# An attention and feed-forward block: instruction orders without an engine loop, with the score chunks of both heads in runs

## Chip, core and metric

The kernel runs on one core of a Trainium2 chip. The metric is the device time in microseconds of one execution of the whole program, all input and weight loads included. Five engines work side by side, each through its own list of instructions: TensorE (PE), VectorE (DVE), ScalarE (ACT), GpSimd (POOL) and SyncE (SP). They wait for each other through semaphores.

## What is computed

The input x is 8 batches of 512 tokens with 256 features, all fp32:

```python
xn = layernorm(x)                                  # over the 256 features
q, k = rope(xn @ wq + bq), rope(xn @ wk + bk)      # 16 heads of 16 features
v = xn @ wv + bv
s = softmax(q @ k.T / 4 + causal mask) @ v @ wo + bo
g = silu((silu(xn @ wg.T) * (xn @ wu.T)) @ wd.T)   # 768 hidden, int32 weights / 127
out = x + s * g
```

For accuracy the kernel splits fp32 operands into a high part (fp32r) and a low part, and multiplies the parts separately.

## The kernel before

The work of each batch is cut into tokens, and for every engine an order of tokens is written out by hand. A token is a kind and an index: `A:3` is score chunk 3. The same token may stand in several engines' lists, and each engine does its own share of it: for `G:0` PE multiplies, ACT takes the tanh and DVE the product.

The kinds that take part below are these. `XT` transposes the normalised input. `QK` and `V` are projections (4 of each a batch), `ROPE` the rotation, `HI` and `LO` the high and low parts of q and k for a pair of heads. `T1q`, `T1k` transpose them into `q_st` and `k_st`. `A` is the first pass of scores of a pair, which DVE reduces to the maximum of each row (L778); `MX` puts the maximum into two more columns of q, `T2` transposes q again, and `B` is the second pass, from which ACT takes the exponential (L668) and POOL masks the diagonal blocks (L869). `PV` multiplies by the values, four heads and four steps, and `ON` normalises. `AT` and `OP` are the output projection, `G`, `U`, `DN` the feed-forward part (6, 6 and 2 a batch), `AD` adds x.

A pair has 6 chunks for each pass: 0 and 1 of 512 columns, 2 and 3 of 384 + 128 (two matmuls), 4 and 5 of 256. Even chunks belong to the first head of the pair, whose operands lie on partitions 0 to 63, odd ones to the second head, on 64 to 127 (`rows` in the matmul tokens, L551 and L562). `A` uses 48 of the 64 rows, `B` all. All other matmuls use all 128 rows; those of `PV` write 32 columns of the array each, four heads side by side.

`SCHEDULE` gives each engine one list of eight lines for a batch, a line for each pair. Kinds in `AHEAD` are shifted by whole pairs: in line s, `A` works on pair s + 1 and `B` on pair s - 1. A token with `>` belongs to the next batch, one with `<` to the batch before. `START` is the list ahead of the first batch.

Every result of PE except that of `PV` goes to one of seven PSUM banks, taken in rotation (`Bank`, `WORK_BANKS`); `take_bank` makes PE wait until the engine that empties the bank has released it. So PE can be at most seven tokens ahead of the slowest reader.

`run` writes plan -1 and plan 0 out, then `Fori` goes three times over plans 1 and 2 with the semaphore values worked out in registers (`need`), and plans 7 and 8 are written out again. SP has a loop of its own for the loads of x and the stores: it loads the x of the next batch behind `XT`, and stores `res` behind `AD`.

The sources of a few lines in the profile: L487 is every matmul of `QK`, `V`, `G`, `U`, `DN` and `OP`, L536 `T1q` and `T1k`, L542 `T2`, L554 `A`, L565 `B`, L580 `PV`, L589 `ON`.

Of the kernel before, what the change touches and what calls it, by code (L numbers as in the profile page):

```python
# [85 lines left out]
START = {
    "pe": """
        WQ XT:0 XT:1 WC V:0 QK:0 V:1 WT:0 QK:1 WT:1 WT:2 QK:2 WT:3 WT:4 V:2 WT:5 WT:6 V:3 QK:3 WT:7 WT:8 WT:9 WT:10 FLAG
        U:0 G:0 G:1 T1q:0 U:1 T1k:0 A:0 A:1 T1k:1 A:2 A:3 A:4 A:5 T1q:1
    """,  # L130
    "act": """
        WQ XT:0 XT:1 WC WT:0 WT:1 WT:2 WT:3 WT:4 WT:5 WT:6 WT:7 WT:8 WT:9 WT:10 G:0 HIq:0 G:1 HIq:1 T1q:0 HIq:2 HL:0
        T1k:0 T1k:1 T1q:1
    """,
    "dve": """
        WQ ST:0 NM:0 NM:1 NM:2 NM:3 XT:0 XT:1 WC V:0 QK:0 ROPE:0 ROPE:1 V:1 ROPE:2 SQ WT:0 ROPE:3 QK:1 ROPE:4 ROPE:5
        WT:1 WT:2 QK:2 ROPE:6 ROPE:7 WT:3 WT:4 V:2 WT:5 V:3 WT:6 WT:7 QK:3 WT:8 FLAG WT:9 WT:10 G:0 LOq:0 U:0 LOk:0 G:1
        U:1 HL:0 LOk:1 LOq:1 A:0 A:1 A:2 LOq:2 A:3 A:4 A:5 MX:0 LOk:2
    """,
    "pool": """  # L140
        WQ RS:0 WC SQ ROPE:8 ROPE:9 ROPE:10 ROPE:11 ROPE:12 ROPE:13 ROPE:14 ROPE:15 HIk:0 HIk:1 HIk:2
# [759 lines left out]
```

## Time and profile before

| | |
|---|---|
| median of 3 runs | 725.07 us (724.32 to 727.4) |
| profiled execution, span | 726.0 us |
| PE busy | 677.4 us, 93% |
| DVE busy | 538.6 us, 74% |
| ACT busy | 411.4 us, 57% |
| POOL busy | 351.7 us, 48% |
| mean granted clock of TensorE | 0.962 |

The profiled execution is one run of the program; its own time is the span of 726.0 us from the first to the last instruction, 0.9 us above the median of the runs and inside their spread. Busy time is time in which an engine works on at least one instruction. The ends of matmuls are modelled, so two neighbouring matmuls may overlap in the record; the distance from one start to the next is the safer measure. PEclk is the share of the full 2.4 GHz that TensorE was granted.

### The profile page before, as it was taken

The page shows a single profiled execution, that of the slowest core. Times are in us where ns is not written, and L with a number is a line of the kernel's source. Part 1 is how long each engine was busy: PE and PEld are TensorE (multiplying, and loading weights), DVE is VectorE, ACT ScalarE, POOL GpSimd, SP SyncE. Part 2 cuts the span into 40 slices and gives each one's busy share as a digit, 9 for nine tenths or more (in the row PEclk, how much of TensorE's full clock was granted, in tenths as well). Part 3 has the DMA queues.
Part 4 walks back from the last instruction along what each step waited for, and adds up shares of the span by engine and source line. Part 5 has one row for each costly group of instructions (what it writes and reads, how often), then busy time and mean ns, then how long its engine had stood idle before and what let it go on. Part 6 is the DMA issues. An engine that isn't in the chain of part 4 may idle for free.

```text
span 726.0 us, 15898 instructions
## 1 busy us (share of the span) xinstructions
PE 677.4 (93%) x4452; PEld 455.3 (63%) x4452; DVE 538.6 (74%) x1735; ACT 411.4 (57%) x897; POOL 351.7 (48%) x697
## 2 busy tenths in 40 slices
PE   1779999999999999899999999899999999999995
PEld 0656766676667665576656766568666766567653
DVE  3779678966978688675889669676697858886663
ACT  2446467756566447464476565555656644765671
POOL 1055493547625674336745476244762567422240
PEclk9888999999999999699999999879999999999898
DMA  8200000000100002000020001100020000100010
GB/s 247 78 1 1 31 1 1 2 3 1 62 28 1 1 1 89 6 1 2 1 89 2 2 1 59 35 2 3 1 74 16 1 1 2 60 1 1 1 60 29
DMA packets 16425, 18.15 MB, mean 25 GB/s; under 512 B 576, under 2 KB 15936, under 8 KB 16320
## 3 DMA queue, kind: packets, MB, share of 16 engines
q1 hardware_dynamic: 15232, 15.86, 6.8%
q8 instruction: 46, 0.75, 0.5%
q10 hardware_dynamic: 1088, 1.05, 0.4%
q14 instruction: 59, 0.48, 0.2%
HBM read 12.71 MB, written 4.19 MB: 23 GB/s over the span
## 4 chain that ended last, share of the span: by engine, by line
PE 84%; DVE 5%; issue 3%; ACT 3%; DMA 2%; POOL 1%; ACTq 0%; DVEq 0%; POOLq 0%
PE ps_w L487 34%; PE ps_w L565 12%; PE ps_w L554 12%; PE ps_o L580 11%; PE ps_w L536 7%; PE ps_w L542 3%; PE ps_w L589 3%; DMA rot<-L_attn_wo 2%; ACT probs L668 1%; PE ps_w L501 1%; ACT o_t L672 1%; DVE ps_w L778 1%; DVE h_lo L719 1%; PE ps_w L595 1%; DVE at_lo L801 1%
## 5 line engine op out<-in xcount | busy, mean ns | idle before, releaser
L778 DVE CUSTOM_DVE_ANT_0 ps_w<-ps_w,cst 128x512 f32<-128x512 f32 (+3 forms) x512 | 242.8, 509 | 54.5 <-PE ps_w L554 52.7
L668 ACT ACTIVATE probs<-ps_w 128x512 f32<-128x512 f32 (+1 forms) x384 | 194.1, 535 | 116.5 <-PE ps_w L565 113.6
L869 POOL TENSOR_SCALAR_AFFINE_SELECT probs<-probs 128x128 f32<-128x128 f32 (+1 forms) x384 | 130.7, 347 | 259.8 <-ACT probs L668 257.4
L565 PE MATMUL ps_w<-q_st,k_st 64*128 64x512 f32 (+3 forms) x512 | 137.9, 375 | 3.7 <-DVE at_lo L801 1.8
L554 PE MATMUL ps_w<-k_st,q_st 48*128 48x512 f32 (+3 forms) x512 | 139.3, 370 | 1.5 <-issue 0.8
L565 PEld LDWEIGHTS ps_w<-q_st,k_st 64*128 64x128 f32 x512 | 72.1, 189 | 52.9 <-issue 29.0
L658 ACT CAST q_st<-ps_w 128x512 fp32r<-128x512 f32 x128 | 74.6, 589 | 51.4 <-PE ps_w L542 39.3
L554 PEld LDWEIGHTS ps_w<-k_st,q_st 48*128 48x128 f32 x512 | 73.6, 189 | 47.3 <-issue 35.4
L487 PE MATMUL ps_w<-xt_hi,wgu_hi 128*128 128x512 f32 x192 | 89.3, 465 | 6.5 <-issue 4.8
L580 PE MATMUL ps_o<-probs,vals 128*32 128x512 f32 (+3 forms) x1024 | 92.5, 451 | 2.0 <-POOL probs L869 2.0
L487 PE MATMUL ps_w<-xt_lo,wgu_hi 128*128 128x512 f32 x192 | 80.7, 420 | 0.0
L778 DVE DVE_READ_ACCUMULATOR2_ANT row_max<- 128x1 f32 x512 | 72.1, 141 | 0.0
L684 ACT ACTIVATE hid<-ps_w 128x512 f32<-128x512 f32 x48 | 28.7, 598 | 54.1 <-PE ps_w L487 36.7
L407 POOL TENSOR_TENSOR rot<-qk_raw,cst 128x512 f32<-128x512 f32 x30 | 38.3, 1278 | 39.4 <-DVE qk_raw L745 32.4
L487 PEld LDWEIGHTS ps_w<-xt_hi,wgu_hi 128*128 128x128 f32 x192 | 38.2, 199 | 29.2 <-issue 18.0
L487 PE MATMUL ps_w<-w_hi,xt_hi 128*128 128x512 f32 (+1 forms) x128 | 50.1, 391 | 6.5 <-DVE w_lo L712 5.1
L814 DVE SCALAR_TENSOR_TENSOR hid<-hid,ps_w 128x512 f32<-128x512 f32 x48 | 32.8, 684 | 28.1 <-ACT hid L684 24.1
L487 PE MATMUL ps_w<-wd_hi,h_hi 128*128 128x256 f32 x192 | 47.9, 292 | 0.0
L658 ACT CAST k_st<-ps_w 128x512 fp32r<-128x512 f32 x64 | 38.5, 601 | 16.1 <-PE ps_w L536 15.9
L412 POOL TENSOR_TENSOR rope_b<-qk_raw,cst 128x256 f32<-128x256 f32 x56 | 47.2, 849 | 0.0
L487 PE MATMUL ps_w<-wd_hi,h_lo 128*128 128x256 f32 x192 | 46.1, 283 | 0.0
L487 PE MATMUL ps_w<-w_lo,xt_hi 128*128 128x512 f32 (+1 forms) x128 | 44.4, 347 | 0.0
(91 smaller groups left out, 1178.2 us busy)
## 6 DMA issues: line engine op xcount, KB each, us to landing
xn<-L_attn_x SPq DMA_DIRECT2D x8, 512.0 KB, 4.8
...
```

Of the source, the lines that this page charges most:

```text
L407: tensor_tensor(by_head(dst), by_head(src), cos, ALU.mult).then_inc(parts, 1)
L412: tensor_tensor(by_two(swapped)[:, :, :, e], by_two(src)[:, :, :, 1 - e], sin[:, :, :, e], ALU.mult).then_inc(parts, 1)
L487: last = pe.matmul(dst, w, m, start=(i == 0), stop=(i == len(terms) - 1))
L536: last = pe.transpose(dst[:, tt * P:(tt + 1) * P].bitcast(F32R), src, ident_r[:])
L554: last = pe.matmul(dst[:, col:col + w], q_st[rows, pair % 2, qt * P:(qt + 1) * P], k_st[rows, pair % 4, 0:w], start=True, stop=True)
L565: last = pe.matmul(dst[:, col:col + w], k_st[rows, pair % 4, kt * P:(kt + 1) * P], q_st2[rows, pair % 2, kt * P:SEQ], start=True, stop=True)
L580: last = pe.matmul(ps_o[32 * hh:32 * hh + 32, kt * P:SEQ], vals[:, b % 2, kt, head * VW:head * VW + 32], probs[:, (hh // 2) * SLOTS + slot ...
L658: nc.scalar.copy(dst, w_of(item)[:, :]).then_inc(ready, 1)
L668: nc.scalar.activation(probs[:, (pair % 2) * SLOTS + slot, col:col + WIDTH[c]], w_of(item)[:, 0:WIDTH[c]], ACT.Exp, scale=QSCALE).then_inc ...
L778: last = nc.vector.tensor_tensor_reduce(out=w_of(item)[:, col:col + w], in0=w_of(item)[:, col:col + w], in1=cst[:, C_MASK + SEQ - w:C_MASK ...
L814: nc.vector.scalar_tensor_tensor(out=hid[:, i % 2, :], in0=hid[:, i % 2, :], scalar=1.0, in1=w_of(item)[:, :], op0=ALU.add, op1=ALU.mult). ...
L869: nc.gpsimd.affine_select(out=v, in_=v, compare_op=ALU.is_ge, fill=0.0, base=0, pattern=pattern, channel_multiplier=-1).then_inc(masked_do ...
```

## The change

`Fori` is gone from all engines and from SP: all plans are written out, with constants as semaphore values and without the two semaphores that were counted up by waits. `SCHEDULE` has new lists for all engines, with absolute chunk numbers (`A:8` is chunk 2 of pair 1) and with `>>` for the batch after next; `START` now holds nearly the whole first batch. Banks are still taken in rotation over seven. Three waits are new: `G` and `U` 0 of the first batch wait for the first eight weight blocks, `DN` 0 for all, and DVE's first `A` chunk of a pair for the maximum of two pairs ago. Inputs, arithmetic, tiles and the number of instructions that compute are the same.

The lists of ACT, DVE and POOL are cut to the lines that the text speaks of; the list of PE for a batch is complete.

```diff
--- before.py
+++ after.py
-AHEAD = {"B": -1, "T2": 0, "A": 1, "MX": 1, "T1q": 2, "T1k": 2, "HIq": 3, "HIk": 3, "LOq": 3, "LOk": 3}
...
 START = {
     "pe": """
-        WQ XT:0 XT:1 WC V:0 QK:0 V:1 WT:0 QK:1 WT:1 WT:2 QK:2 WT:3 WT:4 V:2 WT:5 WT:6 V:3 QK:3 WT:7 WT:8 WT:9 WT:10 FLAG
-        U:0 G:0 G:1 T1q:0 U:1 T1k:0 A:0 A:1 T1k:1 A:2 A:3 A:4 A:5 T1q:1
+        WQ XT:0 XT:1 WC QK:0 QK:1 QK:2 V:0 V:1 V:2 WT:0 WT:1 QK:3 WT:2 WT:3 WT:4 WT:5 WT:6 V:3 WT:7 T1q:0 T1k:0
+        A:0 A:1 FLAG A:2 A:3 A:4 G:0 A:5 G:1 WT:8 T1q:1 U:0 T1k:1 T1k:2 U:1 T2:0 A:6 WT:9 G:2 T1q:2 A:7 U:2 G:3
+        WT:10 U:3 B:0 B:1 B:2 A:8 A:9 B:3 G:4 T1k:3 A:10 U:4 G:5 A:11 A:12 T1q:3 U:5 XT:0> XT:1> A:13 A:14 B:4
+        B:5 A:15 T2:1 V:0> QK:0> V:1> B:6 B:7 A:16 A:17 B:8 A:18 B:9 T1k:4 QK:1> DN:0 A:19 A:20 A:21 A:22 T1q:4
...
     "dve": """
-        WQ ST:0 NM:0 NM:1 NM:2 NM:3 XT:0 XT:1 WC V:0 QK:0 ROPE:0 ROPE:1 V:1 ROPE:2 SQ WT:0 ROPE:3 QK:1 ROPE:4 ROPE:5
-        WT:1 WT:2 QK:2 ROPE:6 ROPE:7 WT:3 WT:4 V:2 WT:5 V:3 WT:6 WT:7 QK:3 WT:8 FLAG WT:9 WT:10 G:0 LOq:0 U:0 LOk:0 G:1
...
+        WQ ST:0 NM:0 NM:1 NM:2 NM:3 XT:0 XT:1 WC QK:0 ROPE:0 ROPE:1 ROPE:2 QK:1 ROPE:3 ROPE:4 QK:2 ROPE:5 ROPE:6
+        V:0 ROPE:7 V:1 WT:0 V:2 QK:3 SQ WT:1 WT:2 LOk:0 LOq:0 WT:3 FLAG V:3 WT:4 WT:5 LOq:1 WT:6 WT:7 A:0 A:1
...
 SCHEDULE = {
     "pe": """
-        G:2 B:0 B:1 A:0 ON:2< A:1 U:2 B:2 T1q B:3 G:3 A:2 A:3 T1k U:3 PV:12< A:4 B:4 B:5 G:4 T2 A:5 U:4 PV:13< PV:14<
-        B:0 A:0 A:1 B:1 G:5 U:5 T1q A:2 B:2 PV:15< B:3 B:4 T1k A:3 T2 A:4 XT:0> XT:1> A:5 B:5
-        DN:0 V:0> B:0 A:0 B:1 A:1 QK:0> B:2 V:1> A:2 B:3 DN:1 A:3 T1q ON:3< B:4 QK:1> A:4 T2 PV:0 PV:1 A:5 T1k B:5 AT:0< PV:2
-        A:0 B:0 B:1 A:1 AT:1< A:2 B:2 T1k A:3 B:3 T1q QK:2> PV:3 A:4 T2 B:4 B:5 A:5
-        B:0 A:0 V:2> T1q B:1 QK:3> T2 B:2 A:1 B:3 T1k B:4 A:2 V:3> A:3 OP:0< A:4 PV:4 B:5 A:5 OP:1<
-        B:0 ON:0 B:1 PV:5 PV:6 B:2 A:0 B:3 T1q T1k A:1 A:2 A:3 T2 PV:7 B:4 A:4 A:5 B:5
-        ON:1 B:0 A:0 B:1 T1q B:2 A:1 B:3 A:2 PV:8 T2 A:3 A:4 B:4 T1k B:5 A:5 PV:9
-        A:0 B:0 B:1 G:0> A:1 A:2 PV:10 U:0> B:2 B:3 T1k A:3 G:1> B:4 PV:11 U:1> T2 T1q A:4 A:5 B:5
+        A:8> A:9> B:47 A:10> PV:12 PV:13 PV:14 B:0> A:11> A:12> B:1> T1q:3> G:5> U:4> U:5> T2:1> PV:15 B:2> B:3>
+        A:13> A:14> A:15> B:4> XT:0>> XT:1>> T1k:3> DN:0> A:16> B:5> A:17> A:18> ON:3 QK:0>> V:0>> V:1>> T1k:4>
+        B:6> A:19> B:7> B:8> B:9> A:20> A:21> A:22> T1q:4> QK:1>> DN:1> AT:0 T2:2> A:23> B:10> B:11> A:24> PV:0>
+        PV:1> PV:2> B:12> A:25> B:13> A:26> B:14> A:27> A:28> A:29> T1k:5> T1q:5> V:2>> QK:2>> QK:3>> AT:1 T2:3>
+        B:15> A:30> PV:3> B:16> B:17> B:18> B:19> B:20> A:31> A:32> A:33> T1q:6> OP:0 OP:1 V:3>> ON:0> T1k:6>
+        T2:4> A:34> B:21> B:22> PV:4> B:23> A:35> B:24> A:36> B:25> B:26> A:37> PV:5> PV:6> B:27> A:38> T1k:7>
+        T1q:7> T2:5> A:39> A:40> PV:7> B:28> B:29> A:41> A:42> B:30> B:31> T1k:0>> ON:1> B:32> A:43> B:33> A:44>
+        T1q:0>> T2:6> B:34> A:45> A:46> PV:8> PV:9> PV:10> A:47> B:35> A:0>> B:36> A:1>> B:37> B:38> A:2>> A:3>>
+        PV:11> B:39> B:40> A:4>> T1k:1>> T2:7> G:0>> G:1>> U:0>> U:1>> G:2>> ON:2> B:41> A:5>> B:42> T1q:1>>
+        U:2>> T1q:2>> B:43> B:44> A:6>> B:45> A:7>> B:46> T1k:2>> G:3>> U:3>> G:4>> T2:0>>
     """,
     "act": """
...
+        B:39> T2:7> G:0>> B:40> G:1>> T1k:1>> HIq:2>> HL:0>> G:2>> B:41> T1q:1>> B:42> T1q:2>> B:43> HL:1>>
...
     "dve": """
...
+        A:47 A:0> A:1> MX:7 A:2> A:3> ST:0>> G:0> A:4> U:0> G:1> LOq:2> HL:0> U:1> G:2> ON:2 A:5> U:2> A:6>
+        HL:1> MX:0> A:7> HL:2> G:3> U:3> G:4> A:8> A:9> LOq:3> HL:3> A:10> A:11> A:12> MX:1> G:5> U:4> U:5>
...
     "pool": """
...
+        B:21> B:22> B:23> AD:0 HIk:0>> B:24> B:25> AD:1 B:26> HIk:1>> B:27> B:28> B:29> B:30> B:31> B:32> B:33>
...
+def token_of(text):
+    kind, _, index = text.rstrip("<>").partition(":")
+    return kind, text.count(">") - text.count("<"), int(index or 0)
...
+    return [(kind, b + ahead, index) for kind, ahead, index in map(token_of, SCHEDULE[engine].split())]
...
-        return [(kind, 0, int(index or 0)) for kind, _, index in (t.partition(":") for t in START[engine].split())]
+        return [(kind, ahead, index) for kind, ahead, index in map(token_of, START[engine].split())]
...
-        MIDDLE = (BATCH - 2) // 2
-        def need(eng, s, value, per_batch, it, apart=None):
-            if it is not None:
-                assert value > 0
-                wait = eng.wait_ge(s, it * (2 * per_batch) + value)
-                if apart:
-                    wait.then_inc(apart, 1)
-            elif value > 0:
+        def need(eng, s, value):
+            if value > 0:
                 eng.wait_ge(s, value)
         def run(name, eng, do):
-            for item in plan(name, -1) + plan(name, 0):
-                do(item, None)
-            with eng.Fori(0, MIDDLE) as it:
-                for item in plan(name, 1) + plan(name, 2):
-                    do(item, it)
-            for item in plan(name, BATCH - 1) + plan(name, BATCH):
-                do(item, None)
-        def wait_full(eng, name, item, it, apart=None):
-            need(eng, full[name], bank.of[item][1], bank.full_per[name], it, apart)
+            for b in range(-1, BATCH + 1):
+                for item in plan(name, b):
+                    do(item)
+        def wait_full(eng, name, item):
+            need(eng, full[name], bank.of[item][1])
...
-            with sp.Fori(1, BATCH - 1) as b:
+            for b in range(1, BATCH - 1):
...
-                    dst = take_bank(item, it)
+                    if i == 0:
+                        need(pe, xt_ready, (b + 1) * KT)
+                        if b == 0:
+                            pe.wait_ge(wt_ready, 8)
...
+                    if b == 0 and i == 0:
+                        pe.wait_ge(wt_ready, WT_USES)
...
-                    wait_full(dve, "dve", item, it, apart=dve_passed)
+                    if c == 0:
+                        need(dve, max_ready, b * PAIRS + pair - 1)
+                    wait_full(dve, "dve", item)
```

## Rows read from the trace of the kernel before

**Rows 1.** The page, part 1: busy time, share of the span, instructions

```profile
PE 677.4 (93%) x4452; PEld 455.3 (63%) x4452; DVE 538.6 (74%) x1735; ACT 411.4 (57%) x897; POOL 351.7 (48%) x697
```

**Rows 2.** Windows, batches from XT to XT: busy time (instructions), clock, DMA

```profile
147.70:229.70 82.00, 81.12 (x554) 54.32 (x553) 65.08 (x214) 49.74 (x111) 45.73 (x89) 1.00 0.06 21
229.70:319.80 90.10, 86.77 (x553) 57.31 (x553) 65.10 (x214) 49.86 (x111) 45.41 (x89) 0.92 0.06 20
...
401.90:491.80 89.90, 86.68 (x554) 57.87 (x553) 65.21 (x214) 49.94 (x111) 45.10 (x89) 0.92 0.06 20
```

**Rows 3.** Chain of waits at 291 us: start, length, what

```profile
291.48 2.47 issue
```

**Rows 4.** Windows: behind the jump at the head of the loop

```profile
295.00:309.00 14.00, 14.00 (x46) 7.74 (x44) 9.14 (x29) 5.74 (x12) 6.22 (x11) 0.51 0.01 4
```

**Rows 5.** Timeline of PE, 386 to 389 us: start, length, line, operands, matmuls

```profile
386.22 0.54 PE L536 MATMUL ps_w<-ident_r,q_nat 128*128 128x128 f32 x4
386.69 0.50 PE L565 MATMUL ps_w<-q_st,k_st 64*128 64x384 f32 x2
387.12 0.50 PE L487 MATMUL ps_w<-xt_hi,wgu_hi 128*128 128x512 f32 x1
...
388.24 0.50 PE L554 MATMUL ps_w<-k_st,q_st 48*128 48x384 f32 x4
388.67 0.53 PE L536 MATMUL ps_w<-ident_r,k_nat 128*128 128x128 f32 x4
```

**Rows 6.** Timeline of PE, 339 to 343 us, runs of score chunks

```profile
339.53 0.49 PE L554 MATMUL ps_w<-k_st,q_st 48*128 48x512 f32 x1
339.54 0.72 PE L565 MATMUL ps_w<-q_st,k_st 64*128 64x512 f32 x2
339.88 0.40 PE L554 MATMUL ps_w<-k_st,q_st 48*128 48x512 f32 x1
340.20 0.66 PE L595 MATMUL ps_w<-cst,attn 128*128 128x128 f32 x4
...
342.47 0.50 PE L554 MATMUL ps_w<-k_st,q_st 48*128 48x384 f32 x2
342.81 0.45 PE L565 MATMUL ps_w<-q_st,k_st 64*128 64x384 f32 x2
343.19 0.54 PE L536 MATMUL ps_w<-ident_r,q_nat 128*128 128x128 f32 x4
```

**Rows 7.** Timeline of PE, 379 to 381 us: U, T2, T1q in a row

```profile
379.42 0.50 PE L487 MATMUL ps_w<-xt_hi,wgu_hi 128*128 128x512 f32 x1
...
380.45 0.45 PE L542 MATMUL ps_w<-ident_r,q_nat 128*128 128x128 f32 x4
380.74 0.50 PE L536 MATMUL ps_w<-ident_r,q_nat 128*128 128x128 f32 x4
381.17 0.38 PE L554 MATMUL ps_w<-k_st,q_st 48*128 48x256 f32 x2
```

**Rows 8.** Windows: up to the first score chunk, straight code, last stretch

```profile
0.00:50.20 50.20, 24.92 (x116) 20.00 (x117) 29.86 (x62) 17.93 (x30) 12.60 (x22) 0.93 0.38 118
50.20:127.60 77.40, 75.87 (x489) 51.25 (x489) 61.24 (x217) 45.02 (x100) 41.88 (x81) 0.96 0.02 8
635.70:726.00 90.30, 78.52 (x537) 51.37 (x536) 56.85 (x186) 49.72 (x108) 23.83 (x67) 0.92 0.06 19
```

**Rows 9.** Windows: from OP to the next G, no dense work

```profile
359.50:373.00 13.50, 12.93 (x108) 7.44 (x107) 12.84 (x48) 10.05 (x23) 7.58 (x18) 1.00 0.34 108
```

**Rows 10.** The page, part 5: group, operands, count, busy, mean, idle before

```profile
L778 DVE CUSTOM_DVE_ANT_0 ps_w<-ps_w,cst 128x512 f32<-128x512 f32 (+3 forms) x512 | 242.8, 509 | 54.5 <-PE ps_w L554 52.7
```

**Rows 11.** Waits: engine, line, waited for, us in total, times, longest

```profile
DVE ps_w L778 <- PE ps_w L554: 52.7, 63, 1.6
```

**Rows 12.** Windows: before and after a fall of the clock at 680.9 us

```profile
677.50:680.90 3.40, 3.17 (x23) 2.07 (x19) 2.31 (x12) 3.14 (x10) 1.27 (x4) 1.00 0.00 0
680.90:684.30 3.40, 3.40 (x19) 2.64 (x18) 1.41 (x4) 3.32 (x7) 1.83 (x6) 0.50 0.00 0
```

More of the change, by code:

```diff
@@ L142 @@
+        B:24 B:25 B:26 B:27 B:28 B:29 B:30 B:31 HIk:1> HIk:2> B:32 B:33
     """,
@@ L188, in steps @@
+        B:21> B:22> B:23> AD:0 HIk:0>> B:24> B:25> AD:1 B:26> HIk:1>> B:27> B:28> B:29> B:30> B:31> B:32> B:33>
+        HIk:2>>
+    """,
+}
+def token_of(text):
+    kind, _, index = text.rstrip("<>").partition(":")
+    return kind, text.count(">") - text.count("<"), int(index or 0)
 def steps(engine, b):
-    items = []
-    for s, line in enumerate(SCHEDULE[engine].strip().splitlines()):
-        for token in line.split():
-            kind, _, index = token.rstrip("<>").partition(":")
-            index = int(index or 0)
-            if kind in AHEAD:
-                n = b * PAIRS + s + AHEAD[kind]
-                items.append((kind, n // PAIRS, n % PAIRS * (CHUNKS if kind in ("A", "B") else 1) + index))
-            else:
-                items.append((kind, b + token.count(">") - token.count("<"), index))
@@ L214, in __init__ @@
     def __init__(self):
-        self.of, full, kinds, seen = {}, {"act": 0, "dve": 0}, {}, {}
+        self.of, full, kinds, seen, at = {}, {"act": 0, "dve": 0}, {}, {}, 0
         for b in range(-1, BATCH + 1):
-            segment = plan("pe", b)
-            places = [i for i in (steps("pe", b) if b >= 0 else segment) if i[0] in WORK]
-            for item in segment:
+            for item in plan("pe", b):
                 if item[0] in WORK:
                     kind, first = item[0], WORK[item[0]][0]
-                    at = places.index(item) % WORK_BANKS
                     full[first] += 1
@@ L226, in __init__ @@
                     seen[at] = (kind, kinds[kind])
-        middle = [i[0] for i in plan("pe", 2) if i[0] in WORK]
-        self.full_per = {e: sum(WORK[k][0] == e for k in middle) for e in full}
-        self.kind_per = {k: middle.count(k) for k in WORK}
-        for one, two in zip(plan("pe", 1) + plan("pe", 2), plan("pe", 3) + plan("pe", 4)):
-            if one[0] in WORK:
-                a, b = self.of[one], self.of[two]
-                assert a[0] == b[0] and b[1] - a[1] == 2 * self.full_per[WORK[one[0]][0]]
-                assert a[2][0] == b[2][0] and b[2][1] - a[2][1] == 2 * self.kind_per[a[2][0]]
+                    at = (at + 1) % WORK_BANKS
 def build(nc, x, wq, bq, wk, bk, wv, bv, wo, bo, w_gate, w_up, w_down, consts, out):
@@ L414, in rotate, with high_parts @@
             else:
-                need(eng, parts, parts_done, 3 * TT, it)
+                need(eng, parts, parts_done)
                 tensor_tensor(dst, dst, swapped, ALU.add).then_inc(rot_ready, 1)
-        def high_parts(name, eng, copy, passed, item, it):
+        def high_parts(name, eng, copy, item):
             kind, b, i = item
@@ L531, in do @@
                 elif kind in ("T1q", "T1k"):
-                    need(pe, lo_q_ready if kind == "T1q" else lo_k_ready, n + 1, PAIRS, it)
-                    dst = take_bank(item, it)
+                    need(pe, lo_q_ready if kind == "T1q" else lo_k_ready, n + 1)
+                    dst = take_bank(item)
                     for tt in range(TT):
@@ L559, in do @@
                     if c == 0:
-                        need(pe, q_st2_ready, b * PAIRS + pair + 1, PAIRS, it)
-                    dst = take_bank(item, it)
+                        need(pe, q_st2_ready, b * PAIRS + pair + 1)
+                    dst = take_bank(item)
                     for h, kt, col in B_PARTS[c]:
@@ L610, in do @@
                 elif kind in ("G", "U"):
-                    if kind == "G" and i == 0:
-                        need(pe, xt_ready, (b + 1) * KT, KT, it)
-                    dst = take_bank(item, it)
+                    if i == 0:
+                        need(pe, xt_ready, (b + 1) * KT)
+                        if b == 0:
+                            pe.wait_ge(wt_ready, 8)
+                    dst = take_bank(item)
                     w, col = (0 if kind == "G" else 1), slice(i * P, (i + 1) * P)
```

244 lines of the change are left out of this document (126 added, 118 removed).

## The prediction, made before the changed kernel was timed

> **What bounds the kernel now.** The page comes first: PE is busy 93% of the 726.0 us span, DVE 74% [rows 1]. That names the engine, not what it loses. So next the busy times batch by batch: a batch costs 82.0 us, of which PE is busy 81.1 and DVE 65.1; the next costs 90.1, with the same work and the clock at 0.92, and two batches later the same again, 89.9 [rows 2]. The chain of waits shows why: at 291.48 it holds 2.47 us of "issue", one of two such pieces, where the engines jump back to the head of `Fori` [rows 3]; from 295.00 on the granted clock is at 0.51, the lower level (1.2 GHz), for 14 us, in which PE starts 46 matmuls, where a quiet batch starts 554 in 82.0 us [rows 2, 4].
>
> The timeline of PE at the full clock then shows what the order costs. I read it from start to start, since the ends are modelled. One head's score chunk of 384 + 128 = 512 columns, between two full-array groups, takes 386.69 to 387.12, 0.43 us; the chunks of both heads together, 388.24 to 388.67, also take 0.43. Four chunks of 512, two of each head, take 339.53 to 340.20, 0.67. But two chunks of one and the same head, one for each pass, take 342.47 to 343.19, 0.72 [rows 5, 6]. So the heads, on partitions 0-63 and 64-127, run side by side, and a run of score chunks costs a fixed part plus the columns of its busier head: from 0.43 to 0.67 is 0.24 us for 512 more columns, 0.47 ns a column, which leaves 0.43 - 0.24 = 0.19 us fixed. The other groups have such a part too. A transpose group alone takes 386.22 to 386.69, 0.47, and a gate group alone 387.12 to 388.24, 1.12 [rows 5]. U, T2 and T1q in a row take 379.42 to 381.17, 1.75 instead of 1.12 + 0.47 + 0.47 = 2.06 [rows 7]: 0.31 for two boundaries that aren't there, 0.15 each.
>
> **The change, part by part.** *The loop.* The two slow batches are 90.1 - 82.0 and 89.9 - 82.0 above the quiet one [rows 2]; without jumps both excesses go, 8.1 + 7.9 = **-16.0 us**. The register arithmetic of the waits goes too. It lay beside running work (PE is busy 81.1 of 82.0 with it) and I count it as nothing; if it were the 0.9 left over it would be 7 us in all. Its other end is a loss: longer straight code to fetch. The first 77 us after 50.2 are straight code already and PE is busy 75.9 of 77.4 there [rows 8], so nothing here either.
>
> *The order on PE.* Counted in the two order lists over all batches, with the same matmuls in both: runs of score chunks fall from 363 to 167, the columns of the busier head summed over runs from 232,192 to 173,824, runs of full-array groups (G, U, QK, V, DN, OP, all transposes) from 330 to 105, runs of PV from 103 to 73. In a middle batch it is 47 to 20, 29,440 to 21,504, 43 to 12 and 13 to 9.
> - Fixed part of score runs: 196 x 0.19 = -37.2 us.
> - Columns: 58,368 x 0.47 ns = -27.4 us. The trace has no run longer than 7 chunks, so I keep the end at which long runs gain nothing from pairing, 0.
> - Full-array runs: 225 x 0.15 = -33.8 us. The other end: only transposes gain it, and G, QK and DN, which stream long, don't, about a third of it.
> - PV runs: not priced by a row of mine; between 0 and 0.19 (the score run's part) I take the 0.15 of the full-array groups: 30 x 0.15 = -4.5 us.
>
> Together **-102.9 us**; a middle batch loses 27 x 0.19 + 7,936 x 0.47 ns + 31 x 0.15 + 4 x 0.15 = 14.1, so PE alone would take 82.0 - 14.1 = 67.9 us.
>
> *The start.* QK:0 to QK:2 now precede V and all WT, SQ goes behind QK:3 on DVE, and the rotations on POOL start earlier. Before the first score chunk at 50.2 PE is busy only 24.9 us and POOL 12.6 [rows 8]. I take **-5 us**, between 0 and -10; weight conversion (WT) still stands on ACT and DVE, and G:0 and DN:0 have a new wait for it. Behind G:0 wait A:5 and G:1 on PE; WT:7 stands nine tokens ahead on PE, hence no cost, at worst 1 us once.
>
> *Moves without a price.* `A` chunk 0 waits for the maximum of two pairs ago, which the same DVE queue has issued some five chunks earlier. SP issues the same x and res loads and stores, unrolled, behind the same semaphores. AD moves on POOL to behind B:23; ACT's G:0, which needs its result, comes a dozen of B chunks later. The x load is issued after XT and wanted only at the next batch's ST.
>
> *What is late next.* DVE. Between OP and the next G there is no dense work, only score chunks, transposes and PV, and there DVE is already busy 12.8 of 13.5 us, beside PE with 12.9 [rows 9]. Shorter switching can't shorten this stretch. In it PE would do its work in 12.9 x 67.9 / 82.0 = 10.7 us and wait the rest. So a middle batch costs 13.5 + (67.9 - 10.7) = 70.7, say **71 us**: 3.1 us come back in each of six middle batches, **+19 us**. In the last stretch nothing more comes back: it lasts 90.3 us with DVE busy 56.9 [rows 8].
>
> Sum: 726.0 - 16.0 - 102.9 - 5 + 19 = 621. The 726.0 is the span of the profiled execution; the median of the runs is 725.07, so 0.9 comes off: **620 us**.
>
> The Trainium skill, TensorEngine Tiling, section PSUM Bottleneck, speaks against the change: tiling speeds up TensorE but not the emptying of PSUM, which may become the limit. The trace agrees for the stretch without dense work. Were the emptying no limit at all the sum would be 620 - 19 = 601; were it the limit everywhere, it is the first rival.
>
> **The rivals.** *First: DVE's queue holds PE up outside that stretch too.* For: a middle batch gives PE 67.9 and DVE 65.1 us, nearly equal, with 7 banks between them, and an order with many score chunks in a row hands DVE its work in bursts (the four chunks that take PE 0.67 us take DVE 4 x 242.8 / 384 = 2.5 us in L778 alone [rows 10]). In the dense 68.5 us DVE was busy 65.1 - 12.8 = 52.3, 0.76; my 71 wants 52.3 / 57.2 = 0.91. Against: in the attention stretch it reaches 0.95 [rows 9]. If it reaches 0.80, the batch is 13.5 + 65.4 = 78.9, 7.9 more in six batches: 620 + 47 = 667.
>
> *Second: the banks decouple well and DVE never idles.* Then the batch is its 65.1 us: 620 - 6 x 5.9 = 585. For: before the change DVE waited for PE's score chunks 52.7 us in 63 waits, the longest just 1.6 [rows 11], which goes if PE is ahead. Against: PE's 67.9 is above 65.1 unless the fixed parts are larger than I read them.
>
> *Third, on the other side: the clock.* At 677.50 PE is busy 3.17 of 3.40 us, and at 680.90 the clock is down to 0.50 [rows 12], with no gap of the loop's kind ahead of it. If PE, held up by DVE, waits often enough in every batch's stretch without dense work, the clock falls in each. 295.00 to 309.00 shows the price: 46 matmuls, at 554 in 82.0 us worth 6.8 us, took 14 [rows 2, 4], so half of the time at the low clock is lost. To end above 726 it needs 106 us lost, 212 us at the low clock, 26 us of each of eight batches: it decides from the point where the clock, once down, stays down for a third of a batch. With 220 us at the low clock it is 620 + 110 = 730. Against: the same stretch of a quiet batch left the clock at 1.00 [rows 9], and two whole batches passed without a fall.
>
> *Fourth: pairing doesn't happen in long runs,* the 27.4 us stay: 647 less what DVE had taken back, some 640. And that the change doesn't do what it says: unrolled code might stall at fetches as the jumps did; against it stands the straight part [rows 8].
>
> **How the numbers follow.** Forecast (603 to 637) 0.47; first rival 0.25; second 0.17; fourth, with fetch stalls, 0.06; clock 0.05, of which 0.04 ends above 726. The range leaves out half of the second rival's better part and the worst of the first and the clock: **585 to 670**. 0.5% is 3.6 us, about what a measurement of this kernel can tell from none: faster 0.95, same 0.01, slower 0.04.
>
> **What would show it.** Right: no "issue" pieces over 1 us in the chain after the start; at the full clock 0.43 us for a pair of 512-column chunks and about 0.9 for six (three of each head); middle batches of 71 us with DVE busy 65; DVE's wait for L554's chunks down, and PE's idle time before score chunks and transposes ended by DVE up, some 20 us. Wrong: middle batches above 76 with PE idle in the dense part (first rival), at 65 (second), a clock below 0.95 inside middle batches (third), a summed time of score runs of more than 113 us without waits (fourth).

## The result, and the profile after

| | before | after |
|---|---|---|
| median of the runs | 725.93 us (724.32 to 727.4) | **651.51 us** (650.03 to 661.99) |
| profiled execution, span | 726.0 us | 648.3 us |
| mean granted clock | 0.962 | 0.945 |

The ratio is 0.897 (95% interval 0.891 to 0.902): 74 us saved, where 105 were forecast. 620 was 31 us too low, and the time lies inside the range of 585 to 670. The ratio leaves out the one slow run, 661.99 us. The accounts below go by the spans of the profiled executions; these differ by 77.7 us, 3 more than the medians. A run's time is 1.7 us above its span, so the profiled run before was, at 727.7, slower than its median, and the one after, at 650.03, quicker. Against the forecast span of 621 the 648.3 is 27 us too long.

The page of the kernel after, parts 1 and 2, and the group of the first pass's reduction from part 5:

```profile
PE 584.9 (90%) x4452; PEld 435.2 (67%) x4452; DVE 553.3 (85%) x1735; ACT 401.4 (62%) x897; POOL 359.0 (55%) x697
...
DVE  2748999897899979997899979998899988998943
ACT  2413647885568555885568655875568755876771
POOL 1260578555865288465874388464874388522530
PEclk9957998999979998999979999999979999999978
...
L732 DVE CUSTOM_DVE_ANT_0 ps_w<-ps_w,cst 128x512 f32<-128x512 f32 (+3 forms) x512 | 239.5, 514 | 21.0 <-PE ps_w L502 20.4
```

PE works 92 us less than before [rows 1], with the same 4452 matmuls. DVE works 15 us more, in a shorter span. DVE's wait for `A` chunks has fallen from 52.7 to 20.4 us [rows 11].

Windows of three middle batches after, from XT to XT (start and end, length, then PE, PEld, DVE, ACT, POOL busy with instructions, clock, share of the DMA engines, GB/s):

```profile
144.40:218.20 73.80, 71.04 (x553) 53.56 (x552) 66.45 (x212) 48.60 (x111) 46.24 (x88) 0.95 0.07 23
218.20:291.30 73.10, 70.30 (x555) 52.76 (x552) 66.59 (x212) 48.49 (x112) 46.25 (x88) 0.98 0.07 23
291.30:365.20 73.90, 71.03 (x556) 53.71 (x553) 66.53 (x213) 48.69 (x112) 46.27 (x88) 0.95 0.07 23
```

These answer to [rows 2]. The six intervals from batch 1's XT to batch 7's last 72.9 us on average. The first of them holds less work (524 matmuls instead of about 553) and takes 69.7 us; the five full ones average 73.5. The slow batches of 90 are gone, and DVE's busy time has gone up from 65.1 to 66.5. PE and DVE are both near full, so the busy shares alone don't say which of them sets the 72.9.

The waits of the kernel after (who, for whom, us in total, times, longest), and PE's timeline at the place that recurs in every batch, behind `OP`:

```profile
PE ps_w L513 <- DVE vals L702: 9.0, 7, 1.5
PE ps_w L435 <- DVE wgu_lo L708: 7.4, 1, 7.4
PE ps_w L513 <- DVE hid L759: 6.6, 6, 1.1
PE ps_w L502 <- DVE wgu_lo L708: 5.9, 1, 5.9
DVE flag_i L679 <- POOL square L832: 5.7, 1, 5.7
```

```profile
252.52 0.38 PE L513 MATMUL ps_w<-q_st,k_st 64*128 64x256 f32 x1 [1.10 <-DVE hid L759]
252.84 1.07 PE L528 MATMUL ps_o<-probs,vals 128*32 128x512 f32 x8
255.35 0.57 PE L513 MATMUL ps_w<-q_st,k_st 64*128 64x256 f32 x2 [1.45 <-DVE vals L702]
```

Windows around it:

```profile
252.00:256.00 4.00, 2.02 (x14) 0.97 (x16) 3.73 (x9) 1.13 (x5) 2.49 (x4) 0.97 0.00 2
255.80:259.20 3.40, 3.40 (x25) 1.73 (x24) 3.16 (x10) 1.97 (x6) 2.98 (x7) 0.50 0.00 0
```

Two chunks of `B` wait for banks that DVE has not emptied, 1.10 and 1.45 us, while DVE itself is busy 3.73 of 4.00. Then the clock is at its lower level for 3.4 us, in other batches for 6.8. In all it is low for about 72 us of the span (55 before), as the mean clocks of 0.945 and 0.962 also give. Three suspects stand in one place: the order of DVE's work, its amount, and the clock.

### The profile page after: what moved, and what is told of

It is laid out like the page before. It is cut to its first block, busy times and chain, and to the rows that moved or that the text cites. A ratio compares the mean times of both kernels' runs of the same rounds, so it can differ in the third digit from the quotient of the medians.

```text
span 648.3 us, 13260 instructions
## 1 busy us (share of the span) xinstructions
PE 584.9 (90%) x4452; PEld 435.2 (67%) x4452; DVE 553.3 (85%) x1735; ACT 401.4 (62%) x897; POOL 359.0 (55%) x697
## 4 chain that ended last, share of the span: by engine, by line
PE 68%; DVE 20%; issue 5%; ACT 3%; POOL 2%; DMA 2%; ACTq 0%; DVEq 0%; POOLq 0%
PE ps_w L435 30%; PE ps_o L528 10%; PE ps_w L513 8%; PE ps_w L484 7%; PE ps_w L502 7%; DVE ps_w L732 6%; PE ps_w L490 2%; PE ps_w L537 2%; DMA rot<-L_attn_wo 2%; DVE q_nat L739 2%; DVE k_nat L722 2%; DVE hid L759 1%; PE ps_w L449 1%; DVE hid L762 1%; DVE row_max L732 1%
## 5 line engine op out<-in xcount | busy, mean ns | idle before, releaser
L732 DVE CUSTOM_DVE_ANT_0 ps_w<-ps_w,cst 128x512 f32<-128x512 f32 (+3 forms) x512 | 239.5, 514 | 21.0 <-PE ps_w L502 20.4
L620 ACT ACTIVATE probs<-ps_w 128x512 f32<-128x512 f32 (+1 forms) x384 | 188.0, 538 | 52.1 <-PE ps_w L513 42.9
L513 PE MATMUL ps_w<-q_st,k_st 64*128 64x512 f32 (+3 forms) x512 | 112.5, 370 | 16.1 <-DVE vals L702 9.0
L502 PE MATMUL ps_w<-k_st,q_st 48*128 48x256 f32 (+3 forms) x512 | 119.4, 370 | 6.1 <-DVE wgu_lo L708 5.9
L513 PEld LDWEIGHTS ps_w<-q_st,k_st 64*128 64x128 f32 x512 | 68.7, 195 | 51.8 <-issue 20.0
L502 PEld LDWEIGHTS ps_w<-k_st,q_st 48*128 48x128 f32 x512 | 67.4, 195 | 22.6 <-issue 11.3
L435 PE MATMUL ps_w<-xt_hi,wgu_hi 128*128 128x512 f32 x192 | 80.2, 418 | 0.2
L435 PE MATMUL ps_w<-w_hi,xt_hi 128*128 128x512 f32 (+1 forms) x128 | 46.5, 363 | 12.4 <-DVE wgu_lo L708 7.4
L528 PEld LDWEIGHTS ps_o<-probs,vals 128*32 128x32 f32 x1024 | 27.7, 116 | 43.7 <-issue 31.2
L380 POOL CAST k_nat<-rot 128x128 fp32r<-128x128 f32 x128 | 40.8, 348 | 15.6 <-ACT k_st L610 15.4
L435 PE MATMUL ps_w<-w_hi,xt_lo 128*128 128x512 f32 (+1 forms) x128 | 44.0, 344 | 0.0
```

What stands on the lines that cost most here:

```text
L380: copy(nat[:, :, :, at * HD:(at + 1) * HD], rot_of(b, i, which)).then_inc(ready, 1)
L435: last = pe.matmul(dst, w, m, start=(i == 0), stop=(i == len(terms) - 1))
L502: last = pe.matmul(dst[:, col:col + w], q_st[rows, pair % 2, qt * P:(qt + 1) * P], k_st[rows, pair % 4, 0:w], start=True, stop=True)
L513: last = pe.matmul(dst[:, col:col + w], k_st[rows, pair % 4, kt * P:(kt + 1) * P], q_st2[rows, pair % 2, kt * P:SEQ], start=True, stop=True)
L528: last = pe.matmul(ps_o[32 * hh:32 * hh + 32, kt * P:SEQ], vals[:, b % 2, kt, head * VW:head * VW + 32], probs[:, (hh // 2) * SLOTS + slot ...
L620: nc.scalar.activation(probs[:, (pair % 2) * SLOTS + slot, col:col + WIDTH[c]], w_of(item)[:, 0:WIDTH[c]], ACT.Exp, scale=QSCALE).then_inc ...
```

## The experiments

Each set of runs had its own runs of the kernel before (medians 724.74, 731.17 and 727.23 us); ratios are against those.

**1. The loop alone.** The old orders, written out.

```diff
-            for item in plan(name, -1) + plan(name, 0):
-                do(item, None)
-            with eng.Fori(0, MIDDLE) as it:
-                for item in plan(name, 1) + plan(name, 2):
-                    do(item, it)
-            for item in plan(name, BATCH - 1) + plan(name, BATCH):
-                do(item, None)
+            for b in range(-1, BATCH + 1):
+                for item in plan(name, b):
+                    do(item, None)
...
-            with sp.Fori(1, BATCH - 1) as b:
+            for b in range(1, BATCH - 1):
```

> The old order of every engine, with Fori written out on all engines and SP, nothing else changed. If the loop costs only its two jumps with the low clock behind each, this is 16 us below the kernel before (about 710 us), and a middle batch stays at 82.0 us. Rival: the register arithmetic of the waits lay on PE's path too; then the middle batches fall as well, by up to 0.9 us each, and the time goes to about 704. Rival: long straight code stalls at fetches as the jumps did; then there are new pieces of issue over 1 us after the start and less than 10 us are won.

Measured: 710.03 us (709.18 to 711.63), ratio 0.981 (0.975 to 0.986), span 709.9. Two of its middle batches, from XT to XT:

```profile
230.00:311.50 81.50, 80.67 (x542) 53.85 (x538) 62.57 (x210) 48.34 (x108) 45.76 (x88) 0.98 0.07 21
311.50:393.00 81.50, 80.90 (x555) 54.28 (x553) 64.73 (x213) 49.82 (x111) 46.14 (x89) 1.00 0.06 21
```

726.0 - 709.9 = 16.1 us between the two profiled executions is what the loop was worth, as priced; the ratio of the runs gives 14 us, with 10 to 18 for its interval. The slow batches of 90 are 81.6 or 83.1 now; the quiet ones went from 82.0 to between 81.5 and 81.8, so the arithmetic of the waits was worth at most 0.5 us a batch, and the start is no faster (first `A` at 52.7). The rest of the gain, 61.6 us between the spans 709.9 and 648.3, is the order's. So the whole of the missing 27 us (648.3 against the forecast span of 621) lies in the order, its start included.

**2. The flag later.** `FLAG` on PE and DVE from behind `A:1` and `WT:3` to behind `A:4`:

```diff
-        A:0 A:1 FLAG A:2 A:3 A:4 G:0 A:5 G:1 WT:8
+        A:0 A:1 A:2 A:3 A:4 FLAG G:0 A:5 G:1 WT:8
```

> The changed kernel, with the token FLAG (the test whether the weights have low parts) moved on PE and DVE to just before the first G; nothing else moved. In the changed kernel DVE stands 5.7 us at FLAG (42.7 to 48.4) with V:3 and seven WT behind it, and PE stands 5.9 us for a bank at 49.6. If that wait is on the start's path, the first score chunk comes some 5 us earlier and the whole is 5 to 8 us shorter (about 643 to 646), more if the clock comes back earlier than at 57.8. Rival: the wait only moves to PE's FLAG before G:0, or ACT and POOL set the pace there; then less than 2 us.

Measured: 650.35 us (649.22 to 658.62), ratio 0.902 (0.894 to 0.911). The first `A` chunk came at 44.5 us instead of 49.6, and batch 1's XT 2.8 us earlier, but PE then stood 3.8 us at the flag, and the last stretch took 138.2 us instead of 136.2. The middle batches stayed at 72.9. Nothing measurable is left at the end.

**3. DVE's order behind OP.** `V:3` ahead of `OP`, and both sums of `OP` ahead of both products:

```diff
-        ... A:32> A:33> OP:0 OP:1
-        LOk:7> ON:0> V:3>> A:34> ...
+        ... A:32> A:33> V:3>> OP:0 OP:1
+        LOk:7> ON:0> A:34> ...
...
-                    need(dve, sum_ready, 2 * b + i + 1)
-                    nc.vector.scalar_tensor_tensor(out=hid[:, i, :], ...)
+                    if i == 1:
+                        need(dve, sum_ready, 2 * b + 2)
+                        for j in range(2):
+                            nc.vector.scalar_tensor_tensor(out=hid[:, j, :], ...)
```

> The changed kernel, but DVE empties the banks of V:3, OP:0 and OP:1 first: V:3 ahead of OP on DVE, and both sums of OP before its two products. In the changed kernel PE stands 1.1 and 1.45 us for these banks in every batch and the clock falls behind it for 3.4 or 6.8 us. If the wait for these banks causes the fall and both are on the path, the gaps go, the clock stays up in the middle batches and a batch is 2 to 3 us shorter: 14 to 20 us in all, about 633. Rival: DVE sets the pace there and is busy all through; then PE's gap only moves, the batch stays within 0.7 us of 73.3 and the total within 5 us, also where the clock stays up.

Measured: 654.44 us (651.71 to 657.27), ratio 0.903 (0.897 to 0.910). The two gaps of PE became one of 1.7 us, some microseconds later. Four middle batches took 72.2 to 73.6 us; two took 78, those in which the clock was low for 17.1 us. So the order of DVE's work moves the gap and does not remove it. What it is worth apart from the two long falls this run doesn't separate: its last stretch, from batch 7's XT on, took 133.4 us instead of 136.2.

**4. What a run of score chunks costs, by itself.** A kernel of its own: the listed patterns 16 or 24 times, without any wait (0 and 1 are 512-column matmuls on partitions 0-63 and 64-127, F a transposing group of four 128-column matmuls over the full array).

```python
PATTERNS = [("full", 24), ("F", 24), ("0 F", 24), ("0 1 F", 24), ("0 0 F", 24), ("0 1 0 1 F", 24), ("0 0 1 1 F", 24),
            ("0 1 0 1 0 1 0 1 F", 16), ("0 0 0 0 1 1 1 1 F", 16), ("0 0 0 0 0 0 0 0 F", 16), ("full", 24), ...]
```

> A kernel of its own that measures PE alone: no other engine reads PSUM, and it leaves out all of the reference's computation. fp32r matmuls in repeated patterns at the full clock: score chunks of 512 columns on partitions 0-63 (0) and 64-127 (1), transposelike groups F of four 128-column full-array matmuls, and full groups of four 512-column ones. By my price (0.19 us a run plus 0.47 ns a column of the busier head, 0.15 us for each run of full-array groups): the score part of 0 F and of 0 1 F is 0.43 us, of 0 1 0 1 F 0.67, of eight chunks alternating 1.15; F alone is 0.32 and 0.47 with a boundary. In 0 0 1 1 F, in order, the heads overlap only in the middle, about 0.91; eight of one head take 2.1. Rival: in long runs the heads do not go on overlapping (weight loads take the port), and eight alternating take over 1.5.

Windows of "0 1 F", "0 0 F", "0 1 0 1 F" (24 times each), eight alternating, eight as 00001111, eight of one head (16 times each):

```profile
86.36:128.76 42.40, 42.40 (x146) 29.07 (x145) 0.00 (x0) 0.00 (x0) 0.50 0.00 0
128.76:181.40 52.64, 52.64 (x146) 34.19 (x146) 0.00 (x0) 0.00 (x0) 0.50 0.00 1
181.40:234.20 52.80, 52.80 (x194) 34.34 (x193) 0.00 (x0) 0.00 (x0) 0.50 0.00 0
287.00:335.74 48.74, 48.74 (x193) 33.28 (x192) 0.00 (x0) 0.00 (x0) 0.50 0.00 0
335.74:384.70 48.96, 48.96 (x193) 33.90 (x192) 0.00 (x0) 0.00 (x0) 0.50 0.00 1
384.70:460.62 75.92, 75.92 (x193) 54.17 (x193) 0.00 (x0) 0.00 (x0) 0.50 0.00 0
```

A pattern takes 1767, 2193, 2200, 3046, 3060 and 4745 ns (the windows divided by the counts). Each further 512 columns of the busier head are 423 to 433 ns at the lower level. Half of 426, 213, is taken for the full clock: 0.42 ns a column, where the prediction read 0.47. The second head is free ("0 F" takes 1767 ns at the lower level, as "0 1 F" does), and the order inside the run makes next to no difference: 3046 and 3060. At the full clock "0 F" takes 1016 ns from start to start (only its first repeats had it) and F alone 448. That leaves 1016 - 448 - 213 = 355 ns for the two boundaries between score chunk and full array; the prediction had 0.19 + 0.15 = 0.34. The fourth rival is out.

**5. The gap filled.** PE does `B:21` three times and `PV:4` twice, so that it has no gap behind `OP`.

```diff
-                    for h, kt, col in B_PARTS[c]:
+                    for h, kt, col in B_PARTS[c] * (3 if i == 21 else 1):
...
-                    for hh in range(4):
+                    for hh in [0, 1, 2, 3] * (2 if i == 4 else 1):
```

> The changed kernel; chunk B:21 is issued three times over and PV:4 twice, with the same operands into the same place, so that PE has something to do ahead of the two waits of 1.1 and 1.45 us that it has in every batch. 0.4 and 1.0 us more of PE's work a batch. If the clock falls behind these waits because PE does too little there, the fall goes in the middle batches, and what a fall costs comes back: 1.7 us (3.4 us low) or 3.4 us (6.8 low) a batch, a period of 70.5 to 71.5 and 10 to 15 us in all (about 637). Rival: DVE sets the pace, the clock's fall hides behind it: the clock stays up and the period is 73 all the same. Rival: the fall has another cause, or the filler is not enough: as many low stretches as before, and up to 1.4 us more a batch (about 658).

Measured: 650.91 us (648.57 to 652.34), ratio 0.892 (0.887 to 0.897). A middle batch:

```profile
218.00:291.00 73.00, 71.02 (x566) 53.22 (x564) 66.66 (x213) 48.64 (x112) 45.97 (x88) 1.00 0.08 23
```

No middle batch has a fall of the clock any more, the time at the lower level is halved (about 34 us against 72), and the five full batches take 73.0 or 73.1. In the kernel after, the two with 3.4 us at the lower level behind `OP` took 73.1 and 72.9, so these falls were hidden behind DVE. The three with 6.8 us took 73.8, 73.9 and 74.0, so a fall of that length cost up to 1 us. All of it is 0.4 us a batch on average, and in the time of the whole nothing that the two ratios (0.892 and 0.897) can tell apart. PE's gap and the clock are not what keeps a batch at 73.

**6. The start.** `FLAG` late as in 2, the squares `SQ` on DVE behind `WT:3`, and on GpSimd the maximum over all partitions, `SQ` too, behind `HIk:2`:

```diff
...
-         V:0 ROPE:7 V:1 WT:0 V:2 QK:3 SQ WT:1 WT:2 LOk:0 LOq:0 WT:3 FLAG V:3
+         V:0 ROPE:7 V:1 WT:0 V:2 QK:3 WT:1 WT:2 WT:3 SQ LOk:0 LOq:0 V:3
...
-        WQ RS:0 WC ROPE:8 ROPE:9 ROPE:10 ROPE:11 ROPE:12 ROPE:13 ROPE:14 ROPE:15 HIk:0 HIk:1 SQ HIk:2 HIk:3
+        WQ RS:0 WC ROPE:8 ROPE:9 ROPE:10 ROPE:11 ROPE:12 ROPE:13 ROPE:14 ROPE:15 HIk:0 HIk:1 HIk:2 SQ HIk:3
```

> The changed kernel with the start alone changed: FLAG just before the first G, as before, and on DVE the three weight blocks WT:1 to WT:3 ahead of the squares SQ, on POOL the all-reduce SQ behind HIk:2. In the changed kernel PE stands 7.4 us for the bank of WT:1 at 38.9, 1.5 at 42.4 and 5.9 at 49.6, with the clock at its lower level from 33.9 to 57.8. If these waits make up the start's excess over my forecast, the first XT of batch 1 comes 6 to 10 us earlier than at 74.7 and the whole falls by as much, to about 643. Rival: the rotations on POOL, slowed by DVE's squares (2.8 us instead of 1.3), set the pace: then the first A comes no sooner than 44 and less than 3 us are won.

Measured: 652.97 us (645.54 to 654.27), ratio 0.891 (0.883 to 0.898): no gain that shows, though one of the four runs took 645.54. PE's gap only moved, to 9.74 us before 42.8, with one of 6.19 before 52.7; batch 1's XT came at 75.6 us instead of 74.7. The profiled execution was the slowest of the four and has one batch of 78.1 us, with the clock low for 17.1.

**7. Less work for DVE.** The maximum is taken over the last 128 columns of each block only.

```diff
-                            out=w_of(item)[:, col:col + w], in0=w_of(item)[:, col:col + w], in1=cst[:, C_MASK + SEQ - w:C_MASK + SEQ],
+                            out=w_of(item)[:, col + w - P:col + w], in0=w_of(item)[:, col + w - P:col + w], in1=cst[:, C_MASK + SEQ - P:C_MASK + SEQ],
```

> The changed kernel, leaving out part of the maximum: DVE's reduction of each score piece takes only its last 128 columns. DVE's load falls from 66.5 to about 54 us a batch; PE, ACT and POOL do the same work. If DVE sets PE's pace, the gaps of PE go and a middle batch falls to PE's own 65.5 to 68 us: 620 or below in all. Rival: PE's own work at the clock that it gets is the bound, and the middle batch stays above 71.

**8. Less work for PE.** The terms with `xt_lo` are left out of `G` and `U`.

```diff
-                    terms = [(wgu_hi[:, w, k, col], xt[:, k, :]) for k in range(KT) for xt in (xt_hi, xt_lo)]
+                    terms = [(wgu_hi[:, w, k, col], xt[:, k, :]) for k in range(KT) for xt in (xt_hi,)]
```

> The changed kernel, leaving out the low part of the input in G and U: half of their matmuls, 24 of 512 columns a batch, 5.5 us of PE's time; nothing else changes. If DVE sets the pace all through, a middle batch stays at 70 us or more. If PE is the bound outside the stretch without dense work, as I forecast, it falls by 4 to 5.5 us, to 68, unless the clock falls more often; DVE can't go below its 66.5.

Measured, one run each: 617.17 us (7) and 645.97 us (8). A middle batch of 7, and one of 8:

```profile
285.00:354.00 69.00, 67.75 (x556) 52.01 (x555) 52.96 (x216) 48.46 (x112) 45.70 (x88) 1.00 0.08 25
```

```profile
144.60:217.40 72.80, 67.01 (x528) 48.32 (x529) 66.31 (x213) 48.45 (x111) 45.97 (x88) 1.00 0.07 23
```

These two decide between the engines. With 13.5 us less on DVE the batches take 69.0 us on average, and PE is busy 67.75 of it: here PE is the bound, 1 us above its forecast 67.9. With 24 matmuls less for PE (some 5.5 us at the full clock) the six intervals stay at 72.85 on average. The clock does not hide a gain here: in the batch shown it never fell, PE was busy only 67.0 us, and the batch took 72.8, beside the 73.0 of experiment 5 at the same clock. The work left out lies in `G` and `U`, the dense part, and DVE's 66.3 us held the batch all the same. DVE sets the pace of the whole batch, not only of the stretch behind `OP`.

**9. A piece of DVE's work moved to ScalarE.** The first of the two instructions of `MX`:

```diff
...
+                elif kind == "MX":
+                    need(act, a_taken, (n + 1) * CHUNKS)
+                    nc.scalar.activation(q_nat[:, i % 4, :, :, 3 * HD], row_max[:, i % 2, :, :], ACT.Copy, scale=-1.0).then_inc(max_hi, 1)
...
-                    need(dve, a_taken, (n + 1) * CHUNKS)
-                    nc.vector.tensor_scalar(qn[:, :, :, 3 * HD], mx, -1.0, None, ALU.mult).then_inc(max_hi, 1)
```

`MX` is also put into ScalarE's lists, and on DVE, where the second instruction remains, it moves one token later.

> The first of the two VectorE instructions that put minus the row maximum into the query rows (128x8, 64 in all, 498 ns each beside GpSimd's rotation, 4.0 us of VectorE per middle batch) is done by ScalarE instead (some 0.3 us each, 46 us busy of 73 so far); VectorE keeps the second one, one item later in its order. Nothing is left out. Theory (VectorE sets the pace of the middle batches, 66.5 us busy of 72.9): VectorE falls to about 62.5 and each of the seven batches gets 3 to 4 us shorter, to 69 to 70, near TensorE's own 68.5 to 69 that the run with the short reduce showed; 651 becomes about 625 (620 to 632). Rival (what holds the batches is the latency of the chain of maximum, query transpose, copy and exponential, not VectorE's load): the move adds a hand-over between engines to that chain, so batches stay at 73 or grow to 75, time 650 to 665.

**10. GpSimd's rotation made narrow.**

```diff
+            if b > 1:
+                src, dst, swapped = src[:, 0:2 * HD], dst[:, 0:2 * HD], swapped[:, 0:2 * HD]
+            heads = 2 if b > 1 else 2 * HEADS
...
```

> GpSimd rotates only the first two of 16 head slices from the third batch on (the rest of the rotation is left out there): 17.1 us of GpSimd per batch become some 4. The work of the other engines is unchanged. Theory (VectorE sets the pace, and a part of its 66.5 us is slowness beside GpSimd: 498 ns instead of 230 for the first maximum instruction, 462 and 451 instead of 393 and 363 for the low parts of K and Q): VectorE's busy time falls to about 63 per batch and the batches from the third on to 70 to 71, the first two stay at 73; span about 635. Rival (the sharing costs nothing that matters, or GpSimd's own order holds nobody up): batches stay within 0.5 us of 73, span 645 to 650. Second rival (GpSimd itself was late for others): batches fall though VectorE's busy time doesn't.

**11. Both 9 and 2.**

> As the run before last, and the flag of the weights (VectorE's compare and TensorE's register load) comes after the fifth first-score chunk instead of after VectorE's third weight block. Nothing is left out. If the start gains what it gained alone (first score matmul 44.5 instead of 49.6, next input transposed 2.8 us earlier) and the batches behind it are no longer paced by a VectorE that has to catch up, the time is 2 to 3 us below the other's, 622 or so (616 to 630); if the gap only moves, as it did alone, it is the same within 1 us.

Measured: **9** 626.14 us (624.72 to 626.93), ratio 0.862 (0.858 to 0.867); **10** 630.85 us, one run; **11** 623.53 us (622.14 to 627.29), ratio 0.860 (0.855 to 0.864). Middle batches of 9 and of 10:

```profile
214.30:284.60 70.30, 68.99 (x555) 52.03 (x553) 62.60 (x204) 49.06 (x120) 45.97 (x88) 1.00 0.07 24
```

```profile
215.50:285.30 69.80, 69.03 (x554) 52.08 (x553) 62.66 (x213) 48.45 (x111) 31.99 (x88) 1.00 0.07 24
```

Two quite different edits take the same 3.9 us off DVE, to 62.6, and both bring the batch to 70. Neither has a fall of the clock in its full middle batches; by experiment 5 that accounts for about 0.5 us of the 3.3 to 3.7 a batch. Experiment 10 left DVE's instructions as they were; they ran faster because GpSimd rotated less. DVE's groups in one middle batch that differ (count, busy, mean ns): before, after, and in 10.

```profile
L770 DVE TENSOR_TENSOR k_nat<-rot,k_nat 128x128 fp32r<-128x128 f32 x8 | 3.1, 393 | 0.0
...
L808 DVE SCALAR_TENSOR_TENSOR hid<-hid,gate 128x512 f32<-128x512 f32 x2 | 2.2, 1112 | 0.1
L785 DVE TENSOR_SCALAR q_nat<-row_max 128x8 fp32r<-128x8 f32 x8 | 1.8, 230 | 0.1
```

```profile
L739 DVE TENSOR_SCALAR q_nat<-row_max 128x8 fp32r<-128x8 f32 x8 | 4.0, 498 | 0.0
L722 DVE TENSOR_TENSOR k_nat<-rot,k_nat 128x128 fp32r<-128x128 f32 x8 | 3.7, 462 | 0.0
...
L762 DVE SCALAR_TENSOR_TENSOR hid<-hid,gate 128x512 f32<-128x512 f32 x2 | 2.4, 1194 | 0.1
```

```profile
L742 DVE TENSOR_SCALAR q_nat<-row_max 128x8 fp32r<-128x8 f32 x8 | 2.8, 351 | 0.0
L725 DVE TENSOR_TENSOR k_nat<-rot,k_nat 128x128 fp32r<-128x128 f32 x8 | 2.3, 285 | 0.0
...
L765 DVE SCALAR_TENSOR_TENSOR hid<-hid,gate 128x512 f32<-128x512 f32 x2 | 1.4, 692 | 0.1
```

The groups that change all read SBUF only (maximum, low parts, product). DVE's instructions that read PSUM keep their time: a sum of `OP` takes 678 ns in the kernel after and 680 in 10, while a product with its gate takes 1194 and 692. The timeline of the kernel after shows how:

```profile
250.46 0.86 POOL L360 TENSOR_TENSOR rope_b<-qk_raw,cst 128x256 f32<-128x256 f32 x1
250.90 0.97 DVE L762 SCALAR_TENSOR_TENSOR hid<-hid,gate 128x512 f32<-128x512 f32 x1
252.11 1.27 POOL L364 TENSOR_TENSOR rot<-rot,rope_b 128x512 f32<-128x512 f32 x1
252.50 1.42 DVE L762 SCALAR_TENSOR_TENSOR hid<-hid,gate 128x512 f32<-128x512 f32 x1
```

GpSimd's two instructions end at 251.32 and 253.38, DVE's products at 251.87 and 253.92. DVE ends 0.54 or 0.55 us behind GpSimd both times, though it started at different points of GpSimd's instruction. All twelve such products of the kernel after end 0.54 to 0.56 us behind one; the four of the last stretch that have no rotation beside them take 0.69. The Trainium skill, SBUF — State Buffer, section "SBUF: two separate sides", names such a lock: VectorE with two SBUF inputs, or in a mode that uses both ports, and GpSimd exclude each other for a whole instruction. The traces agree for the product and the low parts, which have two SBUF inputs. The first instruction of `MX` has one; that it takes the lock too is not shown, only that its mean is 498 ns after, 351 in 10 and 230 before. By its 1112 ns the product met the lock in the kernel before as well.

The latency rival of 9 is out. The chain from maximum to exponential got one more hand-over, and the batch became shorter; and in the whole of the kernel after, the transposes `T2`, which need the maximum, had held PE up for 0.2 us:

```profile
PE ps_w L490 <- DVE q_nat L741: 0.2, 1, 0.2
```

11 is 2.6 us below 9, and its expectation had 2 to 3. Five of its six runs lie below the fastest of 9 and the sixth above the slowest, so the gain is likely, not shown. Its profile has batch 1's XT 3.1 us earlier than that of 9. Both beat the kernel after by 25 us and more.

## Why the prediction was near, and where it was off

- **The loop, -16.0.** Right: 16.1 between the spans, 14 by the ratio of the runs (experiment 1).
- **The order on PE, -102.9.** Nearly right as PE's own work: with DVE lightened, in experiment 7, a middle batch takes 69.0 us, of which PE is busy 67.75, and the forecast for PE alone was 67.9. Single prices were a little off both ways: 0.42 instead of 0.47 ns a column, 0.355 instead of 0.34 us for a pair of boundaries. A run of six chunks, three of each head, took 0.95 us in the timeline after, forecast about 0.9.
- **What DVE gives back, +19.** This term was mis-sized, by two things. The batches took 72.9 instead of 71: 6 x 1.9 = 11.4 us. (By the five full ones, 73.5, it is 2.5 a batch or 15 us, and what is left for the rest of the kernel is that much less.) The step that failed is DVE's busy time, taken over from the old order as 65.1. It was 66.5: the first instruction of `MX` rose from 230 to 498 ns and the low parts of k and q from 393 and 363 to 462 and 451, where the new order puts them beside GpSimd's work, and experiment 10 gets 3.9 us back by shortening that work. At the share that the forecast had (65.1 of 71, 0.917) 66.5 gives 72.5; experiment 5, at the full clock, has 73.0, and the falls of 6.8 us account for the step to 73.5. And the reason given, one stretch in which DVE is full, was too narrow: DVE sets the pace of the whole batch. That is the first rival's mechanism. Reckoned as in the prediction, DVE's share outside the 13.5 us was (66.5 - 12.8) / (73.5 - 13.5) = 0.90, where the forecast had 0.91 and the rival 0.80. By the Trainium skill, TensorEngine Tiling, section PSUM Bottleneck, faster tiled matmuls may run into the emptying of PSUM. The traces agree that an engine which empties banks became the limit: 72.8 us with less for PE, 69.0 with less for DVE; but experiments 9 and 10 shorten the batch without touching the emptying, so it is DVE's whole load that counts. That the sum came out so near with so narrow a reason owes something to chance.
- **"In the last stretch nothing more comes back", and the start, -5.** The forecast leaves 621 - 6 x 71 = 195 us for everything outside the middle batches; it took 648.3 - 6 x 72.9 = 211, 16 more. Some 6.5 to 8 us of that are, as far as the runs tell, DVE's pace again in the last stretch from XT on: 136.2 us, against 129.7 and 128.1 in 9 and 11. Most of the rest is the start, where the -5 did not come. The first `A` came at 49.6 instead of 50.2 us, and by then PE had done 17.9 us of work, not 24.9 [rows 8], so 7 us more of it was still to do. The moved `SQ` now runs beside GpSimd's early rotations: two of the three squares took 2.69 us, the first 1.74, and a rotation product on GpSimd 2.8 us instead of 1.3. On PE `V:3` waits 7.4 us for the bank of `WT:1`, which DVE empties only behind the squares, and DVE waits 5.7 us for GpSimd's maximum over all partitions. I had counted tokens there and not DVE's queue. Experiments 2 and 6 don't win it back by moving single tokens; what a better start would be worth stays open.
- **The clock.** It fell in every middle batch, as the third rival's mechanism says, but not at its price of half the time at the lower level: beside the 73.0 us of experiment 5, 3.4 us cost nothing, 6.8 us some 0.8 to 1, and 17.1 us cost 5, in two batches of experiment 3 and one of 6.
- **No stall at fetches.** The sign named for it, no "issue" piece over 1 us in the chain behind the start, holds for experiment 1 (longest 0.57) and not for the kernel after: it has six such pieces, one in each batch behind `OP`, such as this one.

```profile
252.54 1.31 issue
```

But this piece lies inside DVE's second product of `OP`, on record from 252.50 to 253.92 and held up by GpSimd, as shown above. In experiment 10, with the same straight code and a narrow rotation, these pieces are gone and the longest left is 0.78. So they are the lock, not a fetch.
- **PE's waits.** PE's idle time that DVE ended at the two places behind `OP` is 9.0 + 6.6 = 15.6 us, where the prediction looked for some 20.
